# First-layer and second-layer products of an expert FFN issued alternately, three at a time

## The chip, the cores and the metric

The kernel runs on one core of a Trainium2 chip. The metric is the device time of one execution in microseconds; the lower the better. The engines are TensorE (PE in the profile, with PEld for its weight loads), VectorE (DVE), ScalarE (ACT), GpSimd (POOL) and SyncE (SP, which issues the transfers here).

## What is computed

The program is a macaron block on 2 x 1024 tokens of width 128: a mixture-of-experts FFN, an attention over 16 heads, and the same FFN again, each on a layer-normalised input and added to the residual.

```python
x = x + 0.5 * ffn(layernorm(x))
x = x + attn(layernorm(x))
x = x + 0.5 * ffn(layernorm(x))

# ffn, E = 8 experts, the weights of the two best per token normalised to 1
for e in range(E):
    we = sum(w * (idx == e), axis=-1)
    hmid = gelu(flat @ W1[e] + b1[e])          # 128 -> 512
    out_acc += we[:, None] * (hmid @ W2[e] + b2[e])   # 512 -> 128
```

All eight experts are computed for all tokens; a token's weight is zero for six of them.

## The kernel before

An FFN is a chain of units. One unit is one expert on one quarter of the tokens (512 of them), and the code numbers units by an iteration `i`, which holds two experts, and a step `s` from 0 to 7 (`GR` = 4 quarters, 2 experts). `ffn_units` runs `first` for i = 0, then `body` in a hardware loop for i = 1 and 2, then `last` for i = 3. Each of the five engines has such functions of its own, and they meet in semaphores alone.

A unit has two layers, and each layer has four chunks `mc` of 128 hidden values. Every float32 number is held as a high and a low part, so a chunk of a layer is three products that add up in PSUM: low weights by high data, high by low, high by high.

- `hidden(i, s)` (lines 386 to 401) is the first layer of unit s. Chunk mc goes to PSUM bank mc (banks 0 to 3). It waits (`F.lo`) until the same chunk of unit s - 1 has been read out of that bank. The last product of a chunk increments `F.h`.
- ACT (`front`, lines 485 to 496) adds the bias and applies the gelu in place in the bank (line 495). For chunks 2 and 3 it first writes the high part `hhi` as well (line 494).
- DVE (`front`, `chunks`, lines 680 to 696) makes `hhi` for chunks 0 and 1 (line 684) and the low part `hlo` for all four (line 688), which increments `F.lo`.
- `output(i, s)` (lines 403 to 413) is the second layer of unit s. All four chunks, twelve products, add up in one bank of `Y_BANKS` (banks 4, 6, 7 and 5 in turn). Chunk mc waits for `F.lo` of that chunk; the first waits also for `F.scaled`, until the bank's previous content has been evacuated. The last product increments `F.y`.
- DVE's `back(i, s)` (line 711) evacuates the bank: adds b2, multiplies by the gate and increments `F.scaled`. POOL's `add` (line 544) then adds the result to `acc` and increments `F.acc`. In the loop DVE runs `front` three units ahead of `back`: `front(i, s + SKEW)`, then `back(i, s)`.
- Every fourth step ACT converts the next expert's weights to high parts (lines 330 and 331), POOL makes the low parts (lines 334 and 335), and SP loads later weights, biases and gates as buffers come free.

On PE the order is written out by hand: in `body` and `last`, step s issues all of `hidden(i, s + 1)` and then all of `output(i, s)`. In `last`, steps 5 and 6 put four transposes of finished sums (`back_pe`, lines 170 to 177) between the two; these wait for POOL's `add` of steps 4 and 5. DVE's order in `last` is also written out:

```python
front(i, 3); back(i, 0); back(i, 1)
front(i, 4); back(i, 2); back(i, 3)
front(i, 5); back(i, 4)
front(i, 6); residual_dve(dve, m, 0); back(i, 5)
```

Of the kernel before, what the change touches and what calls it, by code (L numbers as in the profile page):

```python
# [11 lines left out]
P = 128  # L12
D = 128
# [3 lines left out]
GR = TOK // 512  # L17
TPG = NT // GR
E, M = 8, 512
MC = M // P  # L20
# [17 lines left out]
def macaron_kernel(nc, x, cst, wqk, wv, wo, wr, br, w1, b1, w2, b2, out):  # L38
    ctx = ExitStack()
    with ctx:  # L40
        def sem(name):
            return ctx.enter_context(nc.semaphore(name))

        def sb(name, shape, dt, stack=ctx):
            return stack.enter_context(nc.sbuf_tensor(name, shape, dt))
# [4 lines left out]
        def bank(b, n=1):  # L50
            return ps[:, b * 512:(b + n) * 512]

        xt = sb("xt", [P, NT, D], F32)
        xhi = sb("xhi", [P, TOK], F32R)
        xlo = sb("xlo", [P, TOK], F32R)
# [16 lines left out]
        w1hi = sb("w1hi", [P, 2, M], F32R)  # L72
        w1lo = sb("w1lo", [P, 2, M], F32R)
        w2hi = sb("w2hi", [P, 2, MC * D], F32R)
        w2lo = sb("w2lo", [P, 2, MC * D], F32R)
# [14 lines left out]
        hhi = sb("hhi", [P, 2, MC, 512], F32R, ffn)  # L90
        xf = sb("xf", [P, TOK], F32, ffn)
        hlo = sb("hlo", [P, 2, MC, 512], F32R, ffn)
# [43 lines left out]
        s_w1lo = sem("s_w1lo")  # L136
# [22 lines left out]
        Y_BANKS = (4, 6, 7, 5)  # L159
# [7 lines left out]
        def warm_pe():  # L167
            nc.tensor.matmul(bank(7), acc[:, 0:P], acc[:, 0:512], start=True, stop=True)  # L168

        def back_pe(pe, n, g):  # L170

            F = ffns[n.k // 2]
            pe.wait_ge(F.acc, A0 + GR * (E - 2) + g + 1)
            for t in range(TPG):
                at = (g * TPG + t) * P
                last = nc.tensor.transpose(bank(back_bank(n, g))[:, t * P:(t + 1) * P], n.src[:, at:at + P], ident)
            last.then_inc(n.back, 1)
# [20 lines left out]
        def forward_pe(pe, n, g):  # L198

            pe.wait_ge(n.xn, g + 1)  # L200
            if g >= 2:
                pe.wait_ge(n.lo, g if n.k == 1 else g - 1)
            elif n.k == 1:
                pe.wait_ge(n.res, g + 1)
            for t in range(TPG):
                last = nc.tensor.transpose(bank(forward_bank(n, g))[:, t * P:(t + 1) * P], xn[:, g % 2, t, :], ident)
            last.then_inc(n.fwd, 1)
# [75 lines left out]
        S0 = L0 = 4  # L283
# [82 lines left out]
        def ffn_units(eng, first, body, last):  # L366
            first()
            with eng.Fori(1, E // 2 - 1) as i:
                body(i)
            last(E // 2 - 1)  # L370
# [5 lines left out]
        def logits_pe(pe, F, g):  # L376
            pe.wait_ge(F.n.x32, g + 1)
            for t in range(g * TPG, (g + 1) * TPG):
                last = nc.tensor.matmul(bank(5)[:, t * E:(t + 1) * E], xf[:, t * P:(t + 1) * P], wr_sb[:, :],  # L379
                                        start=True, stop=True)  # L380
            last.then_inc(F.logit, 1)

        def ffn_pe(pe, F, outproj):
            n = F.n

            def hidden(i, s):
                u, tt = (s // GR) % 2, s % GR
                if F.f == 0 and isinstance(i, int) and i == 0 and s == 0:
                    pe.wait_ge(s_w1lo, 1)
                elif tt == 0:  # L390
                    pe.wait_ge(F.wready, i * 2 + (s // GR + 1))
                if isinstance(i, int) and i == 0 and s < GR:
                    pe.wait_ge(n.lo, tt + 1)
                for mc in range(MC):
                    if not (isinstance(i, int) and i == 0 and s == 0):
                        pe.wait_ge(F.lo, i * 32 + (4 * s + mc - 3 + L0))
                    w = slice(mc * P, (mc + 1) * P)
                    cols = slice(tt * 512, (tt + 1) * 512)
                    nc.tensor.matmul(bank(mc), w1lo[:, u, w], xhi[:, cols], start=True, stop=False)  # L399
                    nc.tensor.matmul(bank(mc), w1hi[:, u, w], xlo[:, cols], start=False, stop=False)  # L400
                    nc.tensor.matmul(bank(mc), w1hi[:, u, w], xhi[:, cols], start=False, stop=True).then_inc(F.h, 1)  # L401

            def output(i, s):
                u = s // GR
                pe.wait_ge(F.scaled, i * 8 + (s + S0 - 3))
                y = bank(Y_BANKS[s % 4])
                for mc in range(MC):
                    pe.wait_ge(F.lo, i * 32 + (4 * s + mc + 1 + L0))
                    w = slice(mc * D, (mc + 1) * D)
                    nc.tensor.matmul(y, w2lo[:, u, w], hhi[:, s % 2, mc, :], start=(mc == 0), stop=False)  # L410
                    nc.tensor.matmul(y, w2hi[:, u, w], hlo[:, s % 2, mc, :], start=False, stop=False)  # L411
                    last = nc.tensor.matmul(y, w2hi[:, u, w], hhi[:, s % 2, mc, :], start=False, stop=(mc == MC - 1))  # L412
                last.then_inc(F.y, 1)

            def first():
                if outproj:
                    outproj(0)
                    outproj(1)
                    forward_pe(pe, n, 0)
                    pe.wait_ge(n.res, 1)  # L420
                    outproj(2)
                    forward_pe(pe, n, 1)
                    pe.wait_ge(n.res, 2)
                    logits_pe(pe, F, 0)
                    logits_pe(pe, F, 1)
                    hidden(0, 0)
                    pe.wait_ge(n.res, 3)
                    outproj(3)
                    forward_pe(pe, n, 2)
                    hidden(0, 1)  # L430
                    pe.wait_ge(n.res, 4)
                else:
                    forward_pe(pe, n, 0)
                    warm_pe()
                    pe.wait_ge(s_cst, 48)
                    logits_pe(pe, F, 0)
                    forward_pe(pe, n, 1)
                    hidden(0, 0)
                    logits_pe(pe, F, 1)
                    hidden(0, 1)  # L440
                    forward_pe(pe, n, 2)
                    pe.wait_ge(F.wready, 1)
                output(0, 0)
                forward_pe(pe, n, 3)
                logits_pe(pe, F, 2)
                hidden(0, 2)
                logits_pe(pe, F, 3)
                output(0, 1)
                hidden(0, 3)
                output(0, 2)  # L450
                hidden(0, 4)
                pe.wait_ge(F.sh, 1)
                output(0, 3)
                hidden(0, 5)
                pe.wait_ge(F.g, 1)
                pe.wait_ge(F.scaled, S0 + 1)
                nc.tensor.transpose(bank(Y_BANKS[0])[:, 0:P], gte[:, :, :].rearrange("p e t -> p (e t)"),
                                    ident).then_inc(F.gT, 1)
                pe.wait_ge(F.gTs, 1)
                output(0, 4)  # L460
                for s in range(5, 2 * GR):
                    hidden(0, s + 1)
                    output(0, s)

            def body(i):
                for s in range(2 * GR):
                    hidden(i, s + 1)
                    output(i, s)

            def last(i):  # L470
                for s in range(2 * GR - 1):
                    hidden(i, s + 1)
                    if s >= 2 * GR - 3:
                        back_pe(pe, F.after, s - 2 * GR + 3)
                    output(i, s)
                if F.after.k == 1:
                    forward_pe(pe, F.after, 0)
                output(i, 2 * GR - 1)

            ffn_units(pe, first, body, last)  # L480

        def ffn_act(act, F):
# [752 lines left out]
        @block.tensor  # L1235
        def _(pe):
            pe.wait_ge(s_warm, 1)
            for _ in range(WARM):
                warm_pe()
            pe.wait_ge(s_id, 16)  # L1240
            ffn_pe(pe, ffns[0], None)
            outproj_group = att_pe(pe)
            ffn_pe(pe, ffns[1], outproj_group)
            back_pe(pe, norms[3], 2)
            finish_pe(pe, norms[3], 3)
# [38 lines left out]
```

## Time and profile before

| what | value |
|---|---|
| median of 3 runs | 784.38 us (782.45 to 784.77) |
| profiled execution | 784.93 us |
| its span, first to last instruction | 783.1 us |
| PE busy | 772.8 us (99%), 3642 products |
| DVE busy | 675.6 us (86%) |
| ACT busy | 615.7 us (79%) |
| POOL busy | 200.1 us (26%) |
| mean granted TensorE clock | 0.997 of full speed |

The first FFN runs to about 198 us of the span, the attention from there to about 590, the second FFN to the end. A busy time is the sum of an engine's instructions; products on PE overlap in the record (each is drawn with its full latency), so the pace of PE is read from the distance between starts, not from durations. In the timeline, a row with "x3" is three instructions merged, and the bracket at its end says how long the engine was idle before it and what released it.

### The profile page before, as it was taken

The numbers are of one execution on the slowest core, as the hardware profiler recorded it, in microseconds if no ns is written. First come the engines' busy times: TensorE is split into PE (matmuls) and PEld (weight loads), VectorE is DVE, ScalarE is ACT, GpSimd is POOL, SyncE is SP. The second block draws the span as 40 slices with busy tenths as digits, with TensorE's granted clock in tenths as the row PEclk, the third lists the DMA queues.
The fourth block names the chain that finished last, engine by engine and source line by source line (L and its number), as shares of the span: only waits on it lengthen the run. The fifth ranks groups of instructions, "written<-read, shape, count | busy, mean of one in ns | idle before, by whom it ended". The sixth has DMA issues, their size and how long they took to land.

```text
span 783.1 us, 11801 instructions
## 1 busy us (share of the span) xinstructions
PE 772.8 (99%) x3642; PEld 464.5 (59%) x3642; DVE 675.6 (86%) x1348; ACT 615.7 (79%) x1018; POOL 200.1 (26%) x261
## 2 busy tenths in 40 slices
PE   9999999999999999999999999999999999999998
PEld 5778888888772333333333332333498788888886
DVE  7897878789768999999999999999547888878886
ACT  4886767676667999999999999999715767776763
POOL 2117523333301111111111112111112046333331
PEclk9999999999999999999999999999999999999999
DMA  7031312110473111111311111120000024101111
GB/s 206 28 112 54 108 54 107 55 54 1 161 280 98 54 55 54 55 54 54 108 55 55 54 55 54 54 82 1 2 1 1 28 112 157 59 40 68 55 54 54
DMA packets 25413, 54.65 MB, mean 70 GB/s; under 512 B 5264, under 2 KB 10768, under 8 KB 23312
## 3 DMA queue, kind: packets, MB, share of 16 engines
q1 hardware_dynamic: 25360, 54.00, 20.4%
q8 instruction: 27, 0.44, 0.2%
q14 instruction: 26, 0.21, 0.1%
HBM read 44.42 MB, written 9.57 MB: 69 GB/s over the span
## 4 chain that ended last, share of the span: by engine, by line
PE 92%; DVE 5%; ACT 2%; issue 1%; POOL 0%; DVEq 0%
PE ps L979 30%; PE ps L967 11%; PE ps L410 7%; PE ps L411 7%; PE ps L399 7%; PE ps L412 7%; PE ps L401 7%; PE ps L400 7%; PE ps L986 4%; PE ps L168 1%; DVE hlo L688 1%; ACT ef L1056 1%; DVE hhi L684 1%; PE ps L379 1%; PE ps L954 1%
## 5 line engine op out<-in xcount | busy, mean ns | idle before, releaser
L1120 DVE TENSOR_SCALAR_CACHE_REDUCE ef<-ps 128x1024 f32<-128x1024 f32 x256 | 307.3, 1214 | 8.2 <-PE ps L967 1.5
L1056 ACT ACTIVATE ef<-ef,nmax 128x1024 f32<-128x1024 f32 x256 | 293.9, 1148 | 10.5 <-DVE ef L1120 3.8
L979 PE MATMUL ps<-ef,vs 128*64 128x512 f32 x1024 | 249.4, 608 | 0.2
L495 ACT ACTIVATE ps<-ps,b_sb 128x512 f32<-128x512 f32 x256 | 169.2, 664 | 88.2 <-PE ps L401 86.2
L688 DVE TENSOR_TENSOR hlo<-ps,hhi 128x512 fp32r<-128x512 f32 x256 | 165.6, 686 | 4.1
L979 PEld LDWEIGHTS ps<-ef,vs 128*64 128x64 f32 x1024 | 62.8, 136 | 121.0 <-issue 108.4
L684 DVE CAST hhi<-ps 128x512 fp32r<-128x512 f32 x128 | 87.7, 685 | 46.8 <-ACT ps L495 46.7
L1164 POOL TENSOR_TENSOR vs<-V,rsum 128x128 f32<-128x128 f32 x128 | 51.1, 400 | 295.9 <-DVE rsum L1126 295.9
L544 POOL TENSOR_TENSOR acc<-acc,ysc 128x512 f32<-128x512 f32 x55 | 70.7, 1288 | 150.8 <-DVE ysc L711 150.1
L399 PE MATMUL ps<-xhi,w1lo 128*128 128x512 f32 x256 | 101.9, 398 | 0.8 <-DVE hlo L688 0.8
L410 PE MATMUL ps<-hhi,w2lo 128*128 128x512 f32 x256 | 100.9, 394 | 0.8 <-DVE gT L762 0.8
L967 PEld LDWEIGHTS ps<-qs,ks 64*128 64x128 f32 x512 | 38.8, 185 | 105.6 <-DVE ef L1120 103.1
L401 PE MATMUL ps<-xhi,w1hi 128*128 128x512 f32 x256 | 100.9, 394 | 0.0
L400 PE MATMUL ps<-xlo,w1hi 128*128 128x512 f32 x256 | 100.9, 394 | 0.0
L411 PE MATMUL ps<-hlo,w2hi 128*128 128x512 f32 x256 | 100.2, 392 | 0.0
L412 PE MATMUL ps<-hhi,w2hi 128*128 128x512 f32 x256 | 99.8, 390 | 0.0
L967 PE MATMUL ps<-qs,ks 64*128 64x512 f32 x512 | 94.8, 444 | 1.8 <-DVE ef L1120 1.5
L494 ACT ACTIVATE hhi<-ps,b_sb 128x512 fp32r<-128x512 f32 x128 | 88.6, 692 | 4.7
L399 PEld LDWEIGHTS ps<-xhi,w1lo 128*128 128x128 f32 x256 | 47.9, 187 | 14.0 <-DVE hlo L688 3.0
L410 PEld LDWEIGHTS ps<-hhi,w2lo 128*128 128x128 f32 x256 | 48.0, 188 | 12.2 <-DVE gT L762 1.5
L401 PEld LDWEIGHTS ps<-xhi,w1hi 128*128 128x128 f32 x256 | 47.9, 187 | 11.8
L412 PEld LDWEIGHTS ps<-hhi,w2hi 128*128 128x128 f32 x256 | 48.1, 188 | 10.5
(102 smaller groups left out, 672.7 us busy)
## 6 DMA issues: line engine op xcount, KB each, us to landing
gb<-gates SPq DMA_DIRECT2D x16, 1024.0 KB, 4.6
qs<-qk_parts SPq DMA_DIRECT2D x32, 256.0 KB, 3.3
ks<-qk_parts SPq DMA_DIRECT2D x32, 256.0 KB, 3.9
w1raw<-in_w SPq DMA_DIRECT2D x16, 256.0 KB, 4.5
w2raw<-in_w SPq DMA_DIRECT2D x16, 256.0 KB, 4.8
qk_parts<-sthi SPq DMA_DIRECT2D x16, 256.0 KB, 2.2
qk_parts<-stlo SPq DMA_DIRECT2D x16, 256.0 KB, 2.7
xt<-in_x SPq DMA_DIRECT2D x4, 256.0 KB, 3.8
```

Of the source, the lines that this page charges most:

```text
L399: nc.tensor.matmul(bank(mc), w1lo[:, u, w], xhi[:, cols], start=True, stop=False)
L400: nc.tensor.matmul(bank(mc), w1hi[:, u, w], xlo[:, cols], start=False, stop=False)
L401: nc.tensor.matmul(bank(mc), w1hi[:, u, w], xhi[:, cols], start=False, stop=True).then_inc(F.h, 1)
L410: nc.tensor.matmul(y, w2lo[:, u, w], hhi[:, s % 2, mc, :], start=(mc == 0), stop=False)
L411: nc.tensor.matmul(y, w2hi[:, u, w], hlo[:, s % 2, mc, :], start=False, stop=False)
L412: last = nc.tensor.matmul(y, w2hi[:, u, w], hhi[:, s % 2, mc, :], start=False, stop=(mc == MC - 1))
L495: nc.scalar.activation(bank(mc), bank(mc), ACT.Gelu, bias=b1_sb[:, u, mc:mc + 1]).then_inc(F.gelu, 1)
L688: nc.vector.tensor_tensor(hlo[:, s % 2, mc, :], bank(mc), hhi[:, s % 2, mc, :].bitcast(F32), ALU.subtract).then_inc(F.lo, 1)
L967: last = nc.tensor.matmul(bank(slot_bank(u) + half), ks[rows, k % 2, m * P:(m + 1) * P], qs[rows, k % 2, half * 512:(half + 1) * 512], sta ...
L979: last = nc.tensor.matmul(bank(6 + half)[x * VD:(x + 1) * VD, :], vs[:, t % VRING, x * VD:(x + 1) * VD], ef[:, (2 * t + x) % ERING, half * ...
L1056: nc.scalar.activation(ef[:, c, :], ef[:, c, :], ACT.Exp, scale=-1.0, bias=nmax[:, c:c + 1], accum_out=esum[:, c:c + 1]).then_inc(s_exp, 1)
L1120: nc.vector.tensor_scalar(ef[:, c, :], bank(slot_bank(u), 2), -1.0, None, ALU.mult, ALU.min, accum_out=nmax[:, c:c + 1]).then_inc(s_max, 1)
```

## The change

The bodies of `hidden` and `output` are cut into `hidden_chunk(i, s, mc)` and `output_chunk(i, s, mc)`, three products each with the waits that belong to them. `hidden` and `output` still exist and call their chunks four times. A new `both(i, s)` issues chunk mc of `hidden(i, s + 1)` and chunk mc of `output(i, s)` in turn, for mc from 0 to 3. `body` uses it in all eight steps, `last` in its first five; the later steps of `last`, and all of `first`, keep the old order. No other engine's code is changed.

```diff
+            def hidden_chunk(i, s, mc):
+                u, tt = (s // GR) % 2, s % GR
+                if F.f == 0 and isinstance(i, int) and i == 0 and s == 0 and mc == 0:
+                    pe.wait_ge(s_w1lo, 1)
+                elif tt == 0 and mc == 0:
+                    pe.wait_ge(F.wready, i * 2 + (s // GR + 1))
...
+                if not (isinstance(i, int) and i == 0 and s == 0):
+                    pe.wait_ge(F.lo, i * 32 + (4 * s + mc - 3 + L0))
...
+            def output_chunk(i, s, mc):
+                u = s // GR
+                if mc == 0:
+                    pe.wait_ge(F.scaled, i * 8 + (s + S0 - 3))
+                pe.wait_ge(F.lo, i * 32 + (4 * s + mc + 1 + L0))
...
+                if mc == MC - 1:
+                    last.then_inc(F.y, 1)
+
             def hidden(i, s):
...
                 for mc in range(MC):
...
+                    hidden_chunk(i, s, mc)
...
+            def both(i, s):
+                for mc in range(MC):
+                    hidden_chunk(i, s + 1, mc)
+                    output_chunk(i, s, mc)
...
             def body(i):
                 for s in range(2 * GR):
-                    hidden(i, s + 1)
-                    output(i, s)
+                    both(i, s)
 
             def last(i):
-                for s in range(2 * GR - 1):
+                for s in range(2 * GR - 3):
+                    both(i, s)
+                for s in range(2 * GR - 3, 2 * GR - 1):
                     hidden(i, s + 1)
                     if s >= 2 * GR - 3:
                         back_pe(pe, F.after, s - 2 * GR + 3)
```

## Rows read from the trace of the kernel before

**Rows 1.** Page, part 1: busy us (share of the span) and instructions.

```profile
PE 772.8 (99%) x3642; PEld 464.5 (59%) x3642; DVE 675.6 (86%) x1348; ACT 615.7 (79%) x1018; POOL 200.1 (26%) x261
```

**Rows 2.** Waits of PE: engine, line <- releaser: us in total, times, longest.

```profile
PE ps L399 <- DVE hlo L688: 0.8, 4, 0.3
```

**Rows 3.** Windows, one step: us, busy by engine, PEclk, DMA share, GB/s.

```profile
104.18:109.72 5.54, 5.54 (x25) 4.50 (x24) 4.53 (x8) 3.72 (x6) 1.29 (x1) 1.00 0.01 0
```

**Rows 4.** Timeline of PE, one loop step: start, duration, instruction.

```profile
104.18 0.39 PE L399 MATMUL ps<-xhi,w1lo 128*128 128x512 f32 x1
...
104.88 0.39 PE L399 MATMUL ps<-xhi,w1lo 128*128 128x512 f32 x1
...
106.98 0.39 PE L410 MATMUL ps<-hhi,w2lo 128*128 128x512 f32 x1
...
108.36 0.39 PE L410 MATMUL ps<-hhi,w2lo 128*128 128x512 f32 x1
...
109.04 0.39 PE L410 MATMUL ps<-hhi,w2lo 128*128 128x512 f32 x1
...
109.72 0.39 PE L399 MATMUL ps<-xhi,w1lo 128*128 128x512 f32 x1
```

**Rows 5.** Timeline of PE, an output chunk at the end of the first FFN.

```profile
192.35 0.40 PE L410 MATMUL ps<-hhi,w2lo 128*128 128x512 f32 x1
...
193.05 0.39 PE L410 MATMUL ps<-hhi,w2lo 128*128 128x512 f32 x1
```

**Rows 6.** Timeline of PE, ACT and DVE, one step from its first product.

```profile
159.58 0.39 PE L399 MATMUL ps<-xhi,w1lo 128*128 128x512 f32 x1
...
160.48 1.36 ACT L495 ACTIVATE ps<-ps,b_sb 128x512 f32<-128x512 f32 x2 [0.68 <-PE ps L401]
...
163.04 0.69 ACT L494 ACTIVATE hhi<-ps,b_sb 128x512 fp32r<-128x512 f32 x1
163.61 0.67 ACT L495 ACTIVATE ps<-ps,b_sb 128x512 f32<-128x512 f32 x1
...
161.18 0.69 DVE L684 CAST hhi<-ps 128x512 fp32r<-128x512 f32 x1 [0.94 <-ACT ps L495]
161.90 0.69 DVE L688 TENSOR_TENSOR hlo<-ps,hhi 128x512 fp32r<-128x512 f32 x1
162.51 0.68 DVE L684 CAST hhi<-ps 128x512 fp32r<-128x512 f32 x1
163.22 1.89 DVE L688 TENSOR_TENSOR hlo<-ps,hhi 128x512 fp32r<-128x512 f32 x3
165.03 0.74 DVE L711 SCALAR_TENSOR_TENSOR ysc<-ps,b_sb,gb 128x512 f32<-128x512 f32 x1
```

**Rows 7.** Timeline of PE, DVE and POOL, last iteration of both FFNs.

```profile
176.20 0.39 PE L399 MATMUL ps<-xhi,w1lo 128*128 128x512 f32 x1
...
181.94 0.75 DVE L711 SCALAR_TENSOR_TENSOR ysc<-ps,b_sb,gb 128x512 f32<-128x512 f32 x1
...
182.78 1.29 POOL L544 TENSOR_TENSOR acc<-acc,ysc 128x512 f32<-128x512 f32 x1 [3.18 <-DVE ysc L711]
...
184.54 0.60 PE L176 MATMUL ps<-consts,acc 128*128 128x128 f32 x4
...
763.16 1.29 POOL L544 TENSOR_TENSOR acc<-acc,ysc 128x512 f32<-128x512 f32 x1 [3.18 <-DVE ysc L711]
...
764.92 0.60 PE L176 MATMUL ps<-consts,acc 128*128 128x128 f32 x4
```

**Rows 8.** Timeline of DVE and PE where the attention begins.

```profile
197.81 0.68 DVE L249 TENSOR_TENSOR xlo<-ps,xhi 128x512 fp32r<-128x512 f32 x1
...
198.63 0.47 PE L929 MATMUL ps<-xhi,wqklo 128*128 128x512 f32 x1 [1.10 <-DVE xlo L249]
```

**Rows 9.** Timeline of POOL and PE, the last expert's weights.

```profile
743.19 1.30 POOL L335 TENSOR_TENSOR w2lo<-w2raw,w2hi 128x512 fp32r<-128x512 f32 x1
...
751.05 0.39 PE L399 MATMUL ps<-xhi,w1lo 128*128 128x512 f32 x1
```

More of the change, by code:

```diff
@@ L384, in ffn_pe @@
             n = F.n
-            def hidden(i, s):
[L387 to L393, printed above, removed]
-                for mc in range(MC):
[L395 to L401, printed above, removed]
+            def hidden_chunk(i, s, mc):
[4 more added lines that the diff above has]
+                    pe.wait_ge(F.wready, i * 2 + (s // GR + 1))
+                if isinstance(i, int) and i == 0 and s < GR and mc == 0:
+                    pe.wait_ge(n.lo, tt + 1)
+                if not (isinstance(i, int) and i == 0 and s == 0):
+                    pe.wait_ge(F.lo, i * 32 + (4 * s + mc - 3 + L0))
+                w = slice(mc * P, (mc + 1) * P)
+                cols = slice(tt * 512, (tt + 1) * 512)
+                nc.tensor.matmul(bank(mc), w1lo[:, u, w], xhi[:, cols], start=True, stop=False)
+                nc.tensor.matmul(bank(mc), w1hi[:, u, w], xlo[:, cols], start=False, stop=False)
+                nc.tensor.matmul(bank(mc), w1hi[:, u, w], xhi[:, cols], start=False, stop=True).then_inc(F.h, 1)
@@ new lines, in output_chunk @@
+            def output_chunk(i, s, mc):
[3 more added lines that the diff above has]
+                pe.wait_ge(F.lo, i * 32 + (4 * s + mc + 1 + L0))
+                y = bank(Y_BANKS[s % 4])
+                w = slice(mc * D, (mc + 1) * D)
+                nc.tensor.matmul(y, w2lo[:, u, w], hhi[:, s % 2, mc, :], start=(mc == 0), stop=False)
+                nc.tensor.matmul(y, w2hi[:, u, w], hlo[:, s % 2, mc, :], start=False, stop=False)
+                last = nc.tensor.matmul(y, w2hi[:, u, w], hhi[:, s % 2, mc, :], start=False, stop=(mc == MC - 1))
+                if mc == MC - 1:
+                    last.then_inc(F.y, 1)
@@ L403, in output @@
+            def hidden(i, s):
+                for mc in range(MC):
+                    hidden_chunk(i, s, mc)
             def output(i, s):
-                u = s // GR
-                pe.wait_ge(F.scaled, i * 8 + (s + S0 - 3))
-                y = bank(Y_BANKS[s % 4])
                 for mc in range(MC):
[L408 to L412, printed above, removed]
@@ L413, in output @@
-                last.then_inc(F.y, 1)
+                    output_chunk(i, s, mc)
+            def both(i, s):
+                for mc in range(MC):
+                    hidden_chunk(i, s + 1, mc)
+                    output_chunk(i, s, mc)
             def first():
```

## Prediction

> **What bounds the kernel now.** I read the page's shares first: PE is busy for 99% of the span [rows 1], so only what PE does, or waits for, can move the end. The list of PE's waits comes next: in 783.1 us the first-layer products waited for the vector engine 0.8 us in total [rows 2], all told a few us; there is no bubble to fill. Then one step of an expert loop, in the table of windows: 5.54 us long, PE busy for all of it, DVE for 4.53, ACT for 3.72, at a granted clock of 1.00 [rows 3]. So PE alone sets the pace there, and DVE, 82% busy, is the engine with the least room.
>
> A step (`body`, `last`) is 24 products: twelve of the first layer (H, lines 399 to 401) for step s+1, then twelve of the second (O, lines 410 to 412) for step s. By their starts H takes 106.98 - 104.18 = 2.80 us, 0.70 per chunk of three; of the four O chunks the first two take 108.36 - 106.98 = 1.38, so 0.69 each, the others 0.68 each [rows 4]. These are spacings; the durations on the page (0.39) overlap.
>
> **The change part by part.** It removes no product and adds none. PE issues no DMA. Waits and increments are the same in number and value. Only PE's order changes, in the eight steps of `body` (run twice) and the first five of `last`: 21 steps in each of two FFNs, 42 in all, 42 x 5.54 = 233 us.
>
> *Products at their new places.* H spaced as now costs nothing; O is open. Now only the first O chunk follows an H chunk; afterwards all four do. The chunks nearest behind H take 0.69, the later ones fall to 0.68 [rows 4]. If that is what following H costs, two chunks gain 0.01 each: 0.02 us a step, 42 x 0.02 = 0.84 us. The bounds: all at 0.68, 0.02 us a step less than now, -0.8 us; all at the 0.70 that one chunk takes late in the first FFN [rows 5], 4 x 0.70 - 2.74 = 0.06 a step, +2.5 us. I take +0.84, from the row nearest in kind.
>
> *The waits in the steady loop.* H(s+1, c) and O(s, c) both wait for the low part lo(s, c), so the wait ahead of O is met once H has gone. What changes is when lo is made. Count from a step's first product [rows 6]. ACT starts on chunk 0 at 160.48 - 159.58 = 0.90; chunks now follow at 0.70 and will follow at 0.70 + 0.685 = 1.385, so ACT starts at 0.90, 2.29, 3.67 and 5.06. For chunk 3 it makes the high part, starts the gelu 0.57 later (163.61 - 163.04), and DVE can start 0.70 after that (161.18 - 160.48): lo3 runs from 6.33 to 7.01. The output's evacuation (`back`) follows 0.60 behind, at 6.93 ((165.03 - 163.22) / 3 is DVE's pitch), takes 0.74, and ends at 7.67, which is 2.13 into the next step. From there, with 0.72 from high to low part and 0.61 to the next: lo0 ends at 3.54, lo1 at 4.87, lo2 (its gelu ends it) at 5.63. PE needs them at 5.54, 6.93, 8.31 and 9.70: 2.0 us to spare at least. Before the change the least is that of lo1, made at 163.22 + 0.63 = 163.85 and asked for at 159.58 + 5.54 + 0.70 = 165.82: 2.0 too. So nothing is gained or lost in the loop, and DVE's 0.94 us of idle time [rows 6] is only spread out.
>
> *What moves with it.* `back` comes 1.5 us later in a step (165.03 - 159.58 = 5.45 becomes 6.93), the last gelu 1.6 (163.61 - 159.58 = 4.03 becomes 5.63). Behind them stand ACT's conversion of the next expert's weights, POOL's low parts of them, and on SP's queue the loads of gates, bias and weights. The tightest of these: POOL ends w2lo at 743.19 + 1.30 = 744.49, and the product that first needs that expert starts at 751.05 [rows 9]; 6.6 us cover 1.6. Gates are loaded into a buffer read more than four steps (22 us) later. Each costs nothing; without cover it would be a stall of PE once per expert.
>
> *The end of each FFN, where the cover breaks.* In `last`, steps 5 and 6 keep the old order: H(6), then four transposes (`back_pe`, line 176), then O(5). The transposes wait for POOL's add of step 4, that for DVE's `back(4)`, and DVE has `front(5)` ahead of it. Now `back(4)` starts at 181.94, 5.74 into step 4 (origin 176.20), as soon as O(4) is done; POOL starts at 182.78 (0.84 later), takes 1.29, ends at 184.07, and PE arrives at 184.54: 0.47 to spare [rows 7]. Afterwards `front(5)` follows an H(5) that is spread over step 4: lo3 ends at 7.01 as above, `back(4)` starts at 6.93, POOL at 7.77, its end is 9.06. From a DVE result (197.81 + 0.68 = 198.49) to the product that waits for it (198.63) is 0.14 us [rows 8], so the transposes start at 9.20 in place of 184.54 - 176.20 = 8.34: PE stalls for 0.86 us. Queued behind them on PE are O(5), H(7) and all that follows, each released by PE's own results, so the delay stays. The second FFN has the same 0.47 us of cover (764.92 - 763.16 - 1.29) [rows 7] and pays the same: 1.7 us in all. POOL's spans are rough, and what a restart costs beyond the 0.14 isn't shown here: 0.6 to 1.1 us each, 1.2 to 2.2 in all. The same steps also hold the thinnest wait of H: two evacuations ahead of `front(5)` (6.93 + 2 x 0.74 = 8.41, 2.87 into the next step) put the end of lo1 at 2.87 + 0.72 + 0.61 + 0.72 + 0.69 = 5.61, lo3 at 7.01, and the old order of H(6) asks for them at 6.24 and 7.64: 0.63 us to spare.
>
> *The clock.* Products switch PSUM banks every three products in H today, at a granted clock of 1.00 with no idle time [rows 3]. The Trainium skill (TensorE: Matmul & The Clock Gate, A second HAM failure mode) says that cycling through banks can leave small gaps between groups, and that the clock then swings between its two levels. By that, the alternation would lose; the trace so far speaks against it, since the step from O to H (109.04 + 0.68 = 109.72) shows no gap [rows 4].
>
> **The sum.** 0.84 + 1.7 = 2.6 us on the profiled execution's own 784.93 (span 783.1, 1.8 around it): 787.5. That execution lies 0.55 above the median of the runs, 784.38, so I predict 784.38 + 2.6 = 786.9.
>
> **The rivals.**
> - *Dearer O chunks.* All at 0.70, with the stalls: 2.5 + 1.7 = 4.2, 788.6. For: the row in the last step [rows 5]. Against: that stretch follows a bubble, the loop doesn't.
> - *The cover holds, not slower.* If DVE gets `back(4)` out 0.9 us earlier than I work out, or O stays at or below its mean spacing, what is left is 0 to 1.7 us: some 785.3. It decides at 0.47 - 0.14 = 0.33 us of delay: a `back(4)` no later than 5.74 + 0.33 = 6.07 into step 4 costs nothing. For: all offsets come from one execution. Against: `back(4)` stands behind lo3 in DVE's order, and lo3 can't precede its gelu.
> - *H speeds up, not slower.* H takes 0.70 where O takes 0.68; if that is due to its runs of twelve and not to its operands, breaking them gives 4 x 0.02 = 0.08 a step, -3.4 + 1.7 = -1.7 us: 782.7; with O at 0.68 as well, -2.5. The point is 0.01 per chunk, which pays for the stalls. Against: H's first chunk behind O takes its 0.70 at once (104.18 to 104.88) [rows 4].
> - *DVE becomes the bound in the loop.* If the spread chunks made lo 2.0 us later than worked out, each 0.1 us beyond that costs 42 x 0.1 = 4.2: 791. Against: 1 us of its step is idle.
> - *The clock falls.* Each 1% of the 233 us at the lower level, half the speed, would add 2.3 us: 789 at 1%. Against: no idle time on PE here.
>
> **How the numbers follow.** Forecast 0.48 (its own range 786.0 to 787.9), dearer O 0.15, cover holds 0.20, H speeds up 0.10, DVE 0.05, clock 0.02. A measurement of this kernel tells about 0.3% from no change, 2.35 us (above 786.7). The forecast lies just beyond: of its 0.48 some 0.28 falls above, which with dearer O and the last two makes 0.50 slower. Half of H's case is beyond the bound on the other side, 0.05 faster. The rest, 0.45, is within. The range takes in the low bound of the O chunks with the small stalls (-0.8 + 1.2: 784.8), most of the cases in which the cover holds, and dearer O with the larger stalls (2.5 + 2.2: 789.1): 784.2 to 789.3.
>
> **What would show it.** Right: a wait of some 0.9 us of line 176 on POOL's add, once per FFN; H chunks still 0.70 apart from O chunks of 0.69, steps of 5.56; no wait on `hlo` inside the loop. Wrong: no wait at line 176; H below 0.69; steps beyond 5.60; waits of line 399 on DVE in every step; a granted clock below 1.00 in the loop.

## The result, and the profile after

The changed kernel takes 786.1 us (median of 15 runs, 784.9 to 788.53) beside 784.71 for the kernel before on the same chip. The ratio, taken from the means of all runs (786.58 and 784.57), is 1.0026, interval 1.0014 to 1.0038: +2.0 us, 1.1 to 3.0; the medians are 1.4 apart. So it is a little slower, at 0.26% just inside the bound of 0.3%; the predicted time was 786.9. The means mix executions with and without a stretch at half the clock (see below): the seven of the kernel after at a mean granted clock of 1.000 took 785.15 us on average, the three of the kernel before at 1.000 (recorded beside the run e5, below) 782.74, which is 2.4 apart.

The profiled execution tells none of that by its span: 783.1 us, the same as before. The stretches inside it do. I cut it, in the timelines of PE, at the first first-layer product of each FFN, at the first product behind the first FFN, and at the row of the last products. Before, start, duration and instruction (the start behind the first FFN is in [rows 8], 198.63):

```profile
11.54 0.48 PE L399 MATMUL ps<-xhi,w1lo 128*128 128x512 f32 x1
...
587.44 0.48 PE L399 MATMUL ps<-xhi,w1lo 128*128 128x512 f32 x1
...
779.29 0.39 PE L187 MATMUL ps<-consts,ysc 128*128 128x128 f32 x2
```

After:

```profile
10.78 0.48 PE L398 MATMUL ps<-xhi,w1lo 128*128 128x512 f32 x1
...
199.09 0.47 PE L943 MATMUL ps<-xhi,wqklo 128*128 128x512 f32 x1 [1.09 <-DVE xlo L249]
...
586.26 0.48 PE L398 MATMUL ps<-xhi,w1lo 128*128 128x512 f32 x1
...
779.27 0.39 PE L187 MATMUL ps<-consts,ysc 128*128 128x128 f32 x2
```

| us | first FFN | attention stage | second FFN | both FFNs |
|---|---|---|---|---|
| before | 187.09 | 388.81 | 191.85 | 378.94 |
| after | 188.31 | 387.17 | 193.01 | 381.32 |

The FFNs, which the change touches, are 2.38 us longer (1.22 and 1.16). The attention stage, which it doesn't touch, happened to be 1.64 shorter, and the first product came 0.76 earlier (10.78, before 11.54): 2.38 - 1.64 - 0.76 = -0.02. The equal spans are an accident of one execution each. The windows show what it was in the attention. Before (us; busy time and instructions of PE, PEld, DVE, ACT and POOL; granted clock, DMA share, GB/s):

```profile
236.90:240.30 3.40, 2.04 (x8) 0.92 (x10) 3.40 (x7) 2.74 (x5) 0.00 (x0) 0.91 0.83 232
240.30:244.00 3.70, 3.70 (x12) 0.91 (x10) 2.20 (x6) 3.15 (x6) 0.40 (x1) 0.62 0.45 157
```

After, the same windows:

```profile
236.90:240.30 3.40, 1.86 (x8) 0.68 (x8) 3.40 (x7) 2.28 (x4) 0.18 (x1) 1.00 0.95 250
240.30:244.00 3.70, 3.70 (x20) 1.07 (x16) 3.70 (x9) 3.70 (x9) 0.47 (x2) 1.00 0.63 187
```

Both have some 1.4 to 1.5 us of idle PE in the first window; then that of before ran at half the clock, 1.2 GHz, for some 3.4 us (the means 0.91 and 0.62 make 0.09 / 0.5 x 3.40 + 0.38 / 0.5 x 3.70), while that of after stayed at 2.4 GHz. The fall is the usual case: of the thirteen kernels profiled here, all but the kernel after and e6 show it in this place, for 3.4 or 6.8 us. So all that follows is read from the FFN stretches, where the granted clock is 1.00 in every profile but that of e8. Between profiles, the parts of them that no edit touches differ by some 0.1 us in all.

The page's shares after, as in [rows 1]:

```profile
PE 771.4 (99%) x3642; PEld 463.8 (59%) x3642; DVE 678.7 (87%) x1348; ACT 617.5 (79%) x1018; POOL 200.7 (26%) x261
```

PE's waits (engine, line <- releaser: us in total, times, longest):

```profile
PE ps L176 <- POOL acc L558: 1.2, 2, 0.6
PE ps L398 <- DVE hlo L702: 0.8, 4, 0.3
```

The second row is the one of [rows 2], unchanged. The first is new: the predicted stall, once per FFN (it counts idle time from the drawn end of the product ahead; the time lost is read from starts, below). One step of the loop, in the table of windows (as in [rows 3]):

```profile
102.10:107.66 5.56, 5.56 (x25) 4.50 (x24) 4.62 (x8) 3.80 (x7) 1.29 (x1) 1.00 0.34 133
```

It is 5.56 us instead of 5.54, with PE busy throughout at a granted clock of 1.00. The same step in the timeline of PE, first product of each chunk:

```profile
102.13 0.40 PE L398 MATMUL ps<-xhi,w1lo 128*128 128x512 f32 x1
...
102.83 0.39 PE L409 MATMUL ps<-hhi,w2lo 128*128 128x512 f32 x1
...
103.52 0.39 PE L398 MATMUL ps<-xhi,w1lo 128*128 128x512 f32 x1
...
104.22 0.39 PE L409 MATMUL ps<-hhi,w2lo 128*128 128x512 f32 x1
...
107.69 0.40 PE L398 MATMUL ps<-xhi,w1lo 128*128 128x512 f32 x1
```

An H chunk (first layer) still takes 0.70, an O chunk (second layer) now always 0.69. The end of the first FFN, in the timelines of PE, DVE and POOL, and that of the second:

```profile
175.80 0.39 PE L398 MATMUL ps<-xhi,w1lo 128*128 128x512 f32 x1
...
182.14 0.69 DVE L702 TENSOR_TENSOR hlo<-ps,hhi 128x512 fp32r<-128x512 f32 x1 [0.31 <-ACT ps L509]
...
182.75 0.74 DVE L725 SCALAR_TENSOR_TENSOR ysc<-ps,b_sb,gb 128x512 f32<-128x512 f32 x1
...
183.57 1.28 POOL L558 TENSOR_TENSOR acc<-acc,ysc 128x512 f32<-128x512 f32 x1 [3.01 <-DVE ysc L725]
...
183.93 0.40 PE L400 MATMUL ps<-xhi,w1hi 128*128 128x512 f32 x1
...
184.91 0.65 PE L176 MATMUL ps<-consts,acc 128*128 128x128 f32 x4 [0.59 <-POOL acc L558]
...
763.52 1.28 POOL L558 TENSOR_TENSOR acc<-acc,ysc 128x512 f32<-128x512 f32 x1 [3.00 <-DVE ysc L725]
...
764.86 0.66 PE L176 MATMUL ps<-consts,acc 128*128 128x128 f32 x4 [0.58 <-POOL acc L558]
```

The last product of H(6) starts at 183.93 and the transposes 0.98 later, where one product's spacing is 0.23: PE lost 0.75 us, and in the second FFN the same. That is 1.5 of the 2.38 us. The four transposes behind the wait then span 0.65 and 0.66 us, where they spanned 0.60 [rows 7]: 0.1 for both. The 42 alternated steps at 0.02 each give 0.84 (0.88 when the starts of all O chunks are summed). Together that is 2.5, which agrees with 2.38 to the 0.1 us between profiles.

### The profile page after: what moved, and what is told of

Same layout as the page of the kernel before. It is cut to its first block, busy times and chain, and to the rows that moved or that the text cites. A ratio compares the mean times of both kernels' runs of the same rounds, so it can differ in the third digit from the quotient of the medians.

```text
span 783.1 us, 11801 instructions
## 1 busy us (share of the span) xinstructions
PE 771.4 (99%) x3642; PEld 463.8 (59%) x3642; DVE 678.7 (87%) x1348; ACT 617.5 (79%) x1018; POOL 200.7 (26%) x261
## 4 chain that ended last, share of the span: by engine, by line
PE 90%; DVE 5%; ACT 2%; issue 1%; POOL 1%; SPq 1%; DMA 1%; DVEq 0%
PE ps L993 30%; PE ps L981 11%; PE ps L410 7%; PE ps L409 7%; PE ps L411 7%; PE ps L398 7%; PE ps L399 7%; PE ps L400 7%; PE ps L1000 4%; DVE hlo L702 1%; ACT ef L1070 1%; PE ps L379 1%; DVE hhi L698 1%; PE ps L968 1%; PE ps L966 1%
## 5 line engine op out<-in xcount | busy, mean ns | idle before, releaser
L702 DVE TENSOR_TENSOR hlo<-ps,hhi 128x512 fp32r<-128x512 f32 x256 | 172.1, 688 | 36.4 <-ACT ps L509 32.2
L410 PEld LDWEIGHTS ps<-hlo,w2hi 128*128 128x128 f32 x256 | 48.1, 188 | 10.8
```

Of the source, the lines that this page charges most:

```text
L702: nc.vector.tensor_tensor(hlo[:, s % 2, mc, :], bank(mc), hhi[:, s % 2, mc, :].bitcast(F32), ALU.subtract).then_inc(F.lo, 1)
```

## Experiments

Theory, from the prediction: two independent costs, dearer O chunks behind H chunks (0.02 us a step) and a stall at the end of each FFN because `back(4)` comes late. Rivals: the 2.4 us are a diffuse cost of the new order; the stall has another cause than DVE's order; H's 0.70 comes from its runs of twelve, or from its operands. All spans below are of both FFNs together, cut as above, from one profiled execution each; the ratios are of the runs to those of the kernel before, beside it on the same chip. Where an interval takes in 1 (e1, e3, e5), the runs alone don't tell the kernel from before.

| kernel | both FFNs, us | against its base | ratio of times to before, interval |
|---|---|---|---|
| e1_loop_only | 379.55 | +0.61 to before | 1.0004, 0.9992 to 1.0016 |
| e2_last_only | 380.77 | +1.83 to before | 1.0019, 1.0007 to 1.0030 |
| e3_back4_first | 379.76 | -1.56 to after | 1.0006, 0.9994 to 1.0017 |
| e8_back4_late | 385.36 | +6.42 to before | one run: 792.13, before 784.76 |
| e4_x_moved | 373.43 | -5.51 to before | 0.9939, 0.9924 to 0.9953 |
| e5_x_shift64 | 378.08 | -0.86 to before | 0.9994, 0.9980 to 1.0008 |
| e7_x_moved_shift64 | 379.61 | +0.67 to before | one run: 784.98, before 784.76 |
| e9_x_near_aligned | 373.52 | -5.42 to before | 0.9925, 0.9908 to 0.9941 |
| e10_x_moved_off128 | 378.08 | -0.86 to before | one run: 783.57, before 785.01 |
| e6_alternate_x_moved | 375.34 | +1.91 to e4_x_moved | 0.9951, 0.9934 to 0.9967 |
| e11_all_three | 373.56 | +0.13 to e4_x_moved | 0.9927, 0.9910 to 0.9943 |

### Half of the change: e1_loop_only, e2_last_only

The first alternates only in `body`, the second only in the first five steps of `last`. Against the kernel after:

```diff
 # e1_loop_only, last(i)
-for s in range(2 * GR - 3):
-    both(i, s)
-for s in range(2 * GR - 3, 2 * GR - 1):
+for s in range(2 * GR - 1):
     hidden(i, s + 1)
 ...
 # e2_last_only, body(i)
-    both(i, s)
+    hidden(i, s + 1)
+    output(i, s)
```

> The alternation in body alone (32 of the 42 steps); all of last in the old order. Theory (a stall behind POOL's add in last, plus dearer O chunks in each alternated step): no wait of line 176 on POOL, the transposes 0.23 us behind the last H product as before; the 32 steps at 5.56 us against 5.54, so 32 x 0.02 = 0.6 us more than before. Rival (the alternation costs by itself in the loop, the wait is a symptom): about as slow as the changed kernel, 2 us or more above before.

> The alternation in the first five steps of last alone (10 of the 42 steps). Theory: both stalls stay at 0.75 us each, 1.5 us, and 10 x 0.02 = 0.2 us of dearer O chunks: 1.7 us above before. Rival (the stall builds up from delays carried through the loop): no wait of line 176, within 0.3 us of before.

Measured: +0.61 and +1.83, together 2.44 where both at once gave 2.38. The 32 steps of e1 cost 0.61 / 32 = 0.019 each; it has no wait at line 176. In e2 the wait is there as in the kernel after (PE's waits):

```profile
PE ps L176 <- POOL acc L559: 1.2, 2, 0.6
```

Ten steps at 0.02, twice 0.75 and 0.1 for the transposes are 1.8 of its 1.83. The two costs are separate and sit where the prediction put them; a diffuse cost would have followed the number of steps, 32 to 10.

### The stall undone and made longer: e3_back4_first, e8_back4_late

e3 is the kernel after with DVE's `back(4)` moved ahead of the last chunk of `front(5)`; e8 is the kernel before, old order of PE throughout, with `back(4)` put behind the first chunk of `front(6)`.

```diff
 # e3_back4_first, DVE's last(i)
-front(i, 5)
-back(i, 4)
+dve.wait_ge(F.y, i * 8 + (5 + Y0 - 1))
+chunks(i, 5, (0, 1, 2))
+back(i, 4)
+chunks(i, 5, (3,))
 # e8_back4_late, DVE's last(i)
 front(i, 5)
+dve.wait_ge(F.y, i * 8 + (6 + Y0 - 1))
+chunks(i, 6, (0,))
 back(i, 4)
-front(i, 6)
+chunks(i, 6, (1, 2, 3))
```

> The changed kernel, with one move on DVE in last: back(4) goes ahead of chunk 3 of front(5) instead of behind it. Theory: back(4) starts behind lo2, about 5.95 us into step 4 instead of 6.95, POOL's add ends at 8.05, the transposes are due at 8.36: no wait, and what is left is the dearer O chunks, 42 x 0.02 = 0.8 us above before. lo3 ends at about 7.3, H(6) asks for it at 7.66: no new wait. Rival (the stall comes from POOL, or moves to H's wait for lo3): 2 us above before, with a wait of H on hlo in step 5.

> The kernel before, PE in the old order, with DVE's back(4) in last moved behind chunk 0 of front(6), which itself is free for DVE at 183.41 in the trace of before. back(4) then starts at about 184.75, POOL ends at 184.75 + 0.82 + 1.29 = 186.86, the transposes start 0.06 later instead of at 184.54: a stall of 2.4 us in each FFN with no alternation at all, 4.8 us in all. Rival (the stall needs the alternated order on PE): no wait of line 176.

e3, the same stretch in the timelines of PE, DVE and POOL:

```profile
176.38 0.39 PE L398 MATMUL ps<-xhi,w1lo 128*128 128x512 f32 x1
...
182.33 0.74 DVE L725 SCALAR_TENSOR_TENSOR ysc<-ps,b_sb,gb 128x512 f32<-128x512 f32 x1
...
183.15 1.30 POOL L558 TENSOR_TENSOR acc<-acc,ysc 128x512 f32<-128x512 f32 x1 [2.01 <-DVE ysc L725]
...
184.75 0.60 PE L176 MATMUL ps<-consts,acc 128*128 128x128 f32 x4
```

`back(4)` starts 5.95 us into step 4 (the prediction's point of no cost was 6.07), POOL is done at 184.45, and the transposes carry no wait. What remains against before is 0.82 us; 42 x 0.02 is 0.84. e8, where the order of PE is the old one, in the same view:

```profile
183.74 0.40 PE L401 MATMUL ps<-xhi,w1hi 128*128 128x512 f32 x1
...
184.16 0.74 DVE L711 SCALAR_TENSOR_TENSOR ysc<-ps,b_sb,gb 128x512 f32<-128x512 f32 x1
...
184.99 1.27 POOL L544 TENSOR_TENSOR acc<-acc,ysc 128x512 f32<-128x512 f32 x1 [5.97 <-DVE ysc L711]
...
186.31 0.66 PE L176 MATMUL ps<-consts,acc 128*128 128x128 f32 x4 [2.17 <-POOL acc L544]
...
772.03 0.66 PE L176 MATMUL ps<-consts,acc 128*128 128x128 f32 x4 [2.17 <-POOL acc L544]
```

The transposes start 2.57 us behind the product ahead of them, so 2.34 us are lost, in both FFNs: 4.68 of the 6.42. So the time at which DVE runs `back(4)` sets the stall, with the new order or without. The other 1.7 us, which weren't foreseen, lie in the first FFN only, behind its stall (windows of e8):

```profile
187.30:190.70 3.40, 3.40 (x10) 2.66 (x9) 0.72 (x2) 0.00 (x0) 0.00 (x0) 0.50 0.00 0
190.70:194.00 3.30, 3.30 (x16) 2.61 (x15) 2.58 (x11) 1.88 (x3) 1.74 (x3) 1.00 0.00 0
...
772.00:776.00 4.00, 3.97 (x20) 3.35 (x21) 2.27 (x4) 0.00 (x0) 0.00 (x0) 1.00 0.24 70
```

After the 2.17-us wait and 1 us of work the clock was granted at half for 3.4 us (10 products, against 16 in the window behind); the second FFN had the same wait and kept 1.00. Of two equal stalls one thus cost 1.7 times its length ((2.34 + 1.7) / 2.34), the other its length.

### What makes an H chunk dearer: e4, e5, e7, e9, e10

In [rows 4] an H chunk takes 0.70, an O chunk 0.68 to 0.69, with products of equal shape. Five kernels keep the order of before and only move the arrays `xhi` and `xlo`, or put unused bytes beside them:

```diff
 # e4_x_moved
-xhi = sb("xhi", [P, TOK], F32R)
-xlo = sb("xlo", [P, TOK], F32R)
 ...
 w2lo = sb("w2lo", [P, 2, MC * D], F32R)
+xhi = sb("xhi", [P, TOK], F32R)
+xlo = sb("xlo", [P, TOK], F32R)
 # around xhi and xlo, at their old place (e5, e9) or that of e4 (e7, e10);
 # n = 16 and m = 16 in e5 and e7, 16 and 48 in e9, 32 and 32 in e10
+gap0 = sb("gap0", [P, n], F32)
 xhi = sb("xhi", [P, TOK], F32R)
 xlo = sb("xlo", [P, TOK], F32R)
+gap1 = sb("gap1", [P, m], F32)
```

> The kernel before, with the tiles xhi and xlo allocated behind the split weights instead of ahead of xn: the same work in the same order, H's data operand at another place in SBUF, and the weights 16 KB lower. What sets H's 0.70 us a chunk against O's 0.68? If it is where the operands lie: H's chunks change by 0.01 us or more, up to 0.02 x 4 x 64 = 5 us less in all. If it is the order of products or the role of the operand: 0.70 as before, and the time within 0.3% of before.

> The kernel before with 64 spare bytes per partition ahead of xhi and 64 behind xlo: x lies 64 bytes further, in the same part of SBUF, everything behind it 128 bytes further. Theory (what counts is the start of H's data operand modulo 128 bytes: 0 before, 64 for hhi and hlo, 64 for x where it was moved): H chunks at 0.68 us, O chunks all at 0.68, some 5 us less than before. Rival (what counts is the part of SBUF, or x and the weights lying in one part): H at 0.70 and the time of before.

> The kernel before with x moved behind the weights and then shifted by 64 bytes, so that it lies at a multiple of 128 bytes again, at the far place. Theory (address modulo 128): H back at 0.70 us per chunk, stage times of before. Rival (place in SBUF): 0.68.

> The kernel before with 64 spare bytes ahead of xhi and 192 behind xlo. Theory, formed on the runs so far: a chunk takes 0.68 us where the start of its data operand and that of its weights differ by a multiple of 256 bytes, and up to 0.70 where they don't (remainders so far: H 192 before, 0 with x moved, 128 with x shifted by 64, 64 with x moved and shifted; O 0 in all but the last of these, where it was 128 and O became slow). Here the remainder is 0 for H and for O, with x in its old part of SBUF: H 0.68, O 0.68, the FFN stages 5.5 us shorter in all, 779.5 or so. Rival (x has to lie behind the weights): H 0.70, within 0.3% of before.

> The kernel before with x moved behind the weights, 128 spare bytes ahead of it and 128 behind. Theory (the difference to the weights' start modulo 256): remainder 128 for H, 0 for O; H at 0.70 again, O at 0.68 to 0.69, stage times as before the move. Rival (the place behind the weights is what counts): H 0.68.

Timelines of PE follow, each the first product of O, of H, and of the next O (of e5 the last two); the differences are the length of four chunks. e4:

```profile
99.77 0.39 PE L410 MATMUL ps<-hhi,w2lo 128*128 128x512 f32 x1
...
102.48 0.39 PE L399 MATMUL ps<-xhi,w1lo 128*128 128x512 f32 x1
...
105.20 0.39 PE L410 MATMUL ps<-hhi,w2lo 128*128 128x512 f32 x1
```

e7:

```profile
100.94 0.40 PE L412 MATMUL ps<-hhi,w2lo 128*128 128x512 f32 x1
...
103.73 0.40 PE L401 MATMUL ps<-xhi,w1lo 128*128 128x512 f32 x1
...
106.49 0.40 PE L412 MATMUL ps<-hhi,w2lo 128*128 128x512 f32 x1
```

e10:

```profile
100.98 0.39 PE L412 MATMUL ps<-hhi,w2lo 128*128 128x512 f32 x1
...
103.72 0.40 PE L401 MATMUL ps<-xhi,w1lo 128*128 128x512 f32 x1
...
106.51 0.39 PE L412 MATMUL ps<-hhi,w2lo 128*128 128x512 f32 x1
```

e5:

```profile
103.32 0.40 PE L401 MATMUL ps<-xhi,w1lo 128*128 128x512 f32 x1
...
106.11 0.39 PE L412 MATMUL ps<-hhi,w2lo 128*128 128x512 f32 x1
```

e9:

```profile
99.74 0.39 PE L412 MATMUL ps<-hhi,w2lo 128*128 128x512 f32 x1
...
102.46 0.39 PE L401 MATMUL ps<-xhi,w1lo 128*128 128x512 f32 x1
...
105.18 0.39 PE L412 MATMUL ps<-hhi,w2lo 128*128 128x512 f32 x1
```

The first theory, that the data's own start address by 128 bytes decides, fell with e5 and e7: e5's H stayed at 2.79 where it was to fall to 2.72, and in e7 O became the slower layer, which it had not foreseen. With the start addresses of the arrays, as the compiled kernels have them, a pattern appears. Take the start of the data operand less that of its weights (`xhi` - `w1hi` for H, `hhi` - `w2hi` for O) and keep the remainder by 256 bytes:

| kernel | H remainder | H, us per four | O remainder | O, us per four |
|---|---|---|---|---|
| before | 192 | 2.80 | 0 | 2.74 |
| e5 | 128 | 2.79 | 0 | 2.74 |
| e10 | 128 | 2.79 | 0 | 2.74 |
| e7 | 64 | 2.76 | 128 | 2.79 |
| e4 | 0 | 2.72 | 0 | 2.72 (2.71 by the rounded starts above) |
| e9 | 0 | 2.72 | 0 | 2.72 |

Both layers run at 2.72 where both remainders are 0. The rule was formed after e4, e5 and e7; e9 and e10 were built to break it, the one with x at its old place and remainder 0, the other at the place of e4 with 128, and both came out by it. The absolute address doesn't decide: e5 and e9 have `xhi` at the same address, 24,768, and differ by 4.6 us over both FFNs; `w1hi` starts at 54,720 before and at 54,976 in e9, the same by 256, and H takes 2.80 and 2.72. Of the powers of two 256 is the one that fits: in e5 the remainder by 128 is 0 for H, which is slow, and in e4 the remainders by 512 are 0 for H and 256 for O, and both are fast. What in the chip makes it so no run shows.

### The change on top: e6_alternate_x_moved, e11_all_three

e6 is the kernel after with the move of e4; e11 is e6 with the move of e3.

> The changed kernel with x moved behind the weights. If the dearer O chunks come from H and O running at two different spacings, and from each passage between them, they vanish where both run at one: steps of 5.44 us, and only the two stalls remain, 1.5 us above the kernel before with x moved (a step is 0.1 us shorter, so the stalls may be 0.1 us longer: the evacuation keeps its length). If the dearer chunks come from the alternation itself: 0.8 us more, 2.3 above it.

> The alternated order with x moved behind the weights and back(4) ahead of chunk 3 of front(5). Theory: with one spacing for H and O the alternation costs nothing, and without the stalls nothing is left of it: FFN stages within 0.3 us of those of the kernel before with x moved, 779.7. Rival (alternation has a gain that the stall and the dearer chunks hid): 1 us or more below that.

One loop step of e6, timeline of PE (first products of H, O, H chunks and of the next step):

```profile
101.18 0.39 PE L398 MATMUL ps<-xhi,w1lo 128*128 128x512 f32 x1
...
101.86 0.39 PE L409 MATMUL ps<-hhi,w2lo 128*128 128x512 f32 x1
...
102.54 0.39 PE L398 MATMUL ps<-xhi,w1lo 128*128 128x512 f32 x1
...
106.62 0.39 PE L398 MATMUL ps<-xhi,w1lo 128*128 128x512 f32 x1
```

Every chunk takes 0.68 and the step 5.44, as in e4 without alternation: the alternation is free in the loop once both layers have the same spacing. Its stall:

```profile
182.26 0.66 PE L176 MATMUL ps<-consts,acc 128*128 128x128 f32 x4 [0.67 <-POOL acc L558]
```

PE is idle 0.08 longer than in the kernel after (0.59), so it loses 0.83. Of e6's +1.91 the stalls are 2 x 0.83 = 1.66, and the longer transposes 0.1; with them gone, in e11, +0.13 is left. So the alternation had no gain that the stalls covered up. e4, e9 and e11 are 0.6 to 0.75% shorter than before, all three through the address.

## Why the prediction was right, step by step

- *No bubble to fill.* Right: PE's waits for `hlo` are the same row before and after, 0.8 us in 4 waits. The loop had nothing to gain from another order.
- *Products at their new places, +0.84.* Right in size: O chunks of 0.69, steps of 5.56, +0.88 by the starts, 0.82 left in e3. The reason given, following an H chunk, was half of it: following a chunk of another spacing. In e6 O follows H as often and costs nothing, so it is the change between 0.70 and 0.68 that costs, and this kernel has it only because of where `xhi` lies.
- *Waits in the steady loop.* Right: none new. DVE is busy for 4.62 us of 5.56 in place of 4.53 of 5.54 and still isn't the bound.
- *The stall at the end of each FFN, 0.86 each.* Right in place, cause and number; 0.75 measured, 0.80 with the longer transposes. Counted from step 4's start at 175.80, `back(4)` starts at 6.95 (predicted 6.93), POOL starts at 7.77 (7.77) and ends at 9.05 (9.06). The mis-sized term is the restart of PE behind it: 184.91 - 184.85 = 0.06, where I took 0.14 from a product that waits for DVE [rows 8]. The due time was 8.36 for 8.34. The 0.11 less is these two; the 0.05 by which the transposes then ran longer was not in the sum.
- *The clock.* Right: 1.00 in the alternated step. The rule of the Trainium skill (TensorE: Matmul & The Clock Gate, A second HAM failure mode), by which cycling through banks can make the clock swing, isn't borne out by this case: banks now change every three products across both layers and the window shows no idle time.
- *The sum, 2.6.* 2.38 in the stretches, 2.0 (1.1 to 3.0) in the runs. The chances put 0.50 on slower by over 0.3% and 0.45 on within, and it came out within, at 0.26%. The forecast lay just beyond that bound, so a sum 0.22 us too large was enough to cross it.
- *H speeds up.* The rival fell as it stood: breaking the runs of twelve left H at 0.70. Its alternative, "its operands", was the truth, and worth twice the whole effect of the change: 5.5 us. I had that difference of 0.02 in [rows 4] and took it as given.
- *The cover holds; dearer O; DVE.* `back(4)` came at 6.95, past the 6.07 from which it costs; O stayed at 0.69; DVE didn't bound. The kernel after puts the point of no cost at 6.95 - 0.75 = 6.20, 0.13 later than the 6.07; e3, at 5.95, has no wait.

## What to carry to other kernels

Where PE is busy for all of a step, a new order of its products can't gain what isn't idle, but it can lose at the seams: look for the place where the new order meets the old one and for the instruction of another engine that is due there, and move that one along (here `back(4)`, 1.56 us). Two groups of products of equal shape that run at different spacings are a lead worth an experiment of their own. Compare stages, not spans, when one clock stretch somewhere else is as large as the effect.

## What the runs showed of the hardware

- The spacing of 128x512 products in fp32r depended on the start of the data less the start of the weights: 0.227 us a product (2.72 / 12) where the remainder by 256 bytes is 0, 0.230 at 64 (e7), 0.233 at 128 or 192. Within a kernel, passing between two spacings cost the faster group some 0.01 us a chunk (O at 0.69 in the kernel after; 0.68 in e6, where both layers have one spacing).
- PE started 0.05 to 0.06 us after the end of POOL's add that it waited for (kernel after, e8), and 0.14 us after a DVE result [rows 8]; POOL's ends are rough in the profile.
- A stretch of 3.4 us at 1.2 GHz in a busy part cost 1.64 us (attention, before against after) and 1.7 us (e8's first FFN). It came behind idle time of PE, but not every time: in two of the four such places shown here the clock stayed at 2.4 GHz.
